# A twelve-stage decoder on one core: four more units per 32-head attention with plain out products

## What is computed

```
queries = rope(q @ Wq)            # 32 heads of 128
keys    = rope(k @ Wk)            # 8 heads of 128, each used by 4 query heads
values  = v @ Wv
scores  = queries @ keys.T / sqrt(128) + mask      # causal in layer 0
ctx     = softmax(scores) @ values
return ctx.reshape(B, S, 32 * 128) @ Wd            # 4096 columns to 512
x = layernorm(x + attention(x, context))
```

## Time and profile before

| | |
|---|---|
| median of 3 runs | 2799.91 us |
| lowest and highest | 2798.87 and 2800.82 us |
| the profiled execution, whole | 2801.92 us |
| its span | 2800.6 us (1.3 us lie around it) |
| mean granted TensorE clock | 0.987 of 2.4 GHz |
| first attention, main loop without a projection job, steps 56 to 66 | about 796 to 869 us |
| second attention, the same steps | about 1781 to 1853 us |

### The profile page before, as it was taken

How to read it: one execution, slowest core, us unless ns; L and a number is a source line. 1 busy time by engine, 2 the same in 40 slices (tenths; PEclk the granted TensorE clock), 3 DMA queues, 4 the chain that set the end, 5 groups by cost and what they waited for, 6 DMA issues and landing times.

```text
span 2800.6 us, 40463 instructions
## 1 busy us (share of the span) xinstructions
PE 2658.8 (95%) x15768; PEld 1764.9 (63%) x15768; DVE 1652.9 (59%) x3113; ACT 852.1 (30%) x2630; POOL 458.7 (16%) x511
## 2 busy tenths in 40 slices
PE   8999999999989899899999999899998898999998
PEld 7855666666665566556666666656774455576664
DVE  3557667776666456466676667664555644344455
ACT  0012222222233355222222222323444412333331
POOL 1022211222202100132122222022211121000002
PEclk9999999999999899999999999999999999999999
DMA  8631011100001100001111100010000010000000
GB/s 181 92 127 41 20 38 38 38 38 16 16 1 38 69 2 2 27 23 38 38 38 38 38 16 16 1 68 31 2 2 27 20 62 27 15 26 1 12 1 31
DMA packets 53821, 94.89 MB, mean 34 GB/s; under 512 B 29408, under 2 KB 38560, under 8 KB 47488
## 3 DMA queue, kind: packets, MB, share of 16 engines
q1 hardware_dynamic: 53632, 92.30, 10.8%
HBM read 83.89 MB, written 8.39 MB: 33 GB/s over the span
## 4 chain that ended last, share of the span: by engine, by line
PE 87%; DVE 7%; ACT 3%; issue 1%; DMA 1%; POOL 0%; DVEq 0%; SPq 0%; POOLq 0%; ACTq 0%
PE banks L628 19%; PE banks L666 13%; PE banks L620 4%; PE banks L687 4%; PE banks L1209 3%; PE banks L710 3%; PE banks L1719 3%; PE banks L303 3%; PE banks L1771 3%; PE banks L2009 2%; PE banks L2041 2%; PE banks L1748 2%; PE banks L2074 2%; PE banks L1724 2%; PE banks L650 2%; PE banks L697 2%
## 5 line engine op out<-in xcount | busy, mean ns | idle before, releaser
L628 PE MATMUL banks<-xT,weights 128*128 128x512 f32 x1024 | 458.2, 592 | 0.0
L748 ACT ACTIVATE E_x<-S_x,sm_x 128x128 f32<-128x128 f32 x512 | 199.3, 390 | 588.1 <-DVE sm_x L837 588.1
L628 PEld LDWEIGHTS banks<-xT,weights 128*128 128x128 f32 x1024 | 188.9, 190 | 209.5 <-issue 206.6
L887 POOL TENSOR_TENSOR QT<-QT,turned 128x512 f32<-128x512 f32 x128 | 162.4, 1269 | 708.2 <-DVE QT L781 506.5
L809 DVE TENSOR_TENSOR x<-banks,x 128x512 f32<-128x512 f32 x336 | 171.5, 510 | 143.7 <-PE banks L666 137.9
L779 DVE TENSOR_TENSOR turned<-banks,const 64x512 f32<-64x512 f32 x160 | 109.4, 684 | 233.1 <-PE banks L628 232.6
L666 PE MATMUL banks<-weights 128*128 128x256 f32 x896 | 223.8, 383 | 0.0
L161 POOL TENSOR_TENSOR norm_spread<-norm_mv,const 128x1 f32<-128x1 f32 x96 | 20.9, 218 | 1223.4 <-DVE norm_mv L157 1223.4
L666 PE MATMUL banks<-weights,OT 128*128 128x256 f32 x672 | 178.1, 387 | 25.1 <-DVE x L809 12.3
L666 PEld LDWEIGHTS banks<-weights 128*128 128x128 f32 x896 | 163.9, 191 | 44.4 <-DVE x L809 15.0
L666 PEld LDWEIGHTS banks<-weights,OT 128*128 128x128 f32 x672 | 120.5, 190 | 79.3 <-DVE x L809 38.8
(11 more groups left out here) (294 smaller groups left out, 4546.8 us busy)
## 6 DMA issues: line engine op xcount, KB each, us to landing
weights<-in_L_xwq SPq DMA_DIRECT2D x16, 1024.0 KB, 4.8
weights<-in_L_xwo SPq DMA_DIRECT2D x16, 1024.0 KB, 7.4
weights<-in_L_xwk SPq DMA_DIRECT2D x16, 256.0 KB, 5.1
weights<-in_L_xwv SPq DMA_DIRECT2D x16, 256.0 KB, 5.4
weights<-in_L_ffn_W_base SPq DMA_DIRECT2D x3, 1024.0 KB, 4.8
weights<-in_L_xwq SPq DMA_DIRECT2D x4, 768.0 KB, 5.0
weights<-in_L_xwo SPq DMA_DIRECT2D x4, 768.0 KB, 6.4
xT<-in_xT SPq DMA_DIRECT2D x4, 512.0 KB, 9.9
```

The source lines that it names most:

```text
L628: mm = PE.matmul(bank[:, :], weight, source[:, k, half_of(i)], start=k == 0, stop=k == KC - 1)
L748: ins = AC.activation(e[:, j, :], s[:, j, :], ACT.Exp, bias=sm[:, 0, j:j + 1], scale=1.0, accum_out=sm[:, 1, j:j + 1])
L887: PO.tensor_tensor(dst, dst, turned[j % 2][:, :, :], ALU.add).then_inc(*x_roped.one())
```

## The change

`pairs` goes from 28 to 26, for both attentions. Units 52 to 55, the last four of group 6, get plain products in steps 55 to 58 instead of the pairs 26 and 27 in steps 56 to 59. The other edits make this hold together: the plain product takes the `wo` buffer of its own group, SP's wait is written by `outs_to` (the same count as before for every group that is loaded), and the row statistics are taken for the last group alone.

```
-                pairs = (units - B) // 2
+                pairs = (units - B) // 2 - 2
...
                         if g >= 2:
-                            SP.wait_ge(*x_out(outs(4 * (g - 1))))
+                            SP.wait_ge(*x_out(outs_to(B * (g - 1) - 1)))
...
                         if u is not None:
-                            PE.wait_ge(*wo_here(G8 - 1))
+                            PE.wait_ge(*wo_here(u // B))
...
                             for h in range(4):
-                                mm = PE.matmul(psum[7][:, :], OT[u // 2 % 2][:, u % 2, h, :], wo[(G8 - 1) % 2][:, h, :], start=h == 0, stop=h == 3)
+                                mm = PE.matmul(psum[7][:, :], OT[u // 2 % 2][:, u % 2, h, :], wo[u // B % 2][:, h, :], start=h == 0, stop=h == 3)
...
                             DV.tensor_tensor(x[:, b, :], psum[7][:, :], x[:, b, :], ALU.add).then_inc(*x_sum.one())
-                            norm.stats(b, x_sum(NA * pairs + b + 1))
+                            if u >= units - B:
+                                norm.stats(b, x_sum(NA * pairs + u - 2 * pairs + 1))
```

## The result

The changed kernel takes 2779.14 us, the median of 6 runs (2775.44 to 2781.93), against 2799.46 us before (6 runs, 2798.87 to 2800.82). The ratio is 0.9925, with a 95% interval of 0.9913 to 0.9938. The direction was right, the size was not.

What follows compares the result with a forecast made beforehand. PE's list of work and its waits were taken to bound the kernel. Savings of 7.73 us in the first attention and 6.23 in the second, 13.96 together, took the median 2799.91 to 2786.0 us, range 2783.5 to 2790.

Steps and rivals of the forecast that it cites:

- The bound: Whole kernel: PE is busy 95% of the span, so the total is its work plus the places where it stands still.
- the place of the wait (L792): Step 56 of both attentions: PE idles 2.85 us until DVE's last sum of `OT`, with no projection job covering it.
- 4.28 us added to step 55: End of step 55: unit 52's plain product makes turn to scores 5.25 us instead of 0.97, so 4.28 us more.
- 22.5 us for steps 56 to 59: Steps 56 to 59, both attentions: four plain steps of 5.62 us each, without idle time on PE.
- no wait for L816: Steps 56 to 59: PE waiting for L816 there would show the forecast wrong; 1.01 us of slack was expected.
- First step that failed: Waits in both attentions: one slow stretch of 1.50 us per run, so 13.96 us saved in all.
- Second step: Clock in later blocks: one slow stretch more or fewer plus 0.5 us for the rest, 2 us either way.
- Half the gain: Rival: the eight new steps last 6.05 us each, giving back 3.4 us, total 2789.4 us; chance 0.10.
- The waits did not come back: Rival judged: steps keep 3.23 us of waits per pair, products cost their columns, total 2803.3 us; chance 0.03.
- chain through bank 7: Rival: new steps run without overlap, 8.94 us each, 12.6 us slower in all, total 2812.5 us; chance 0.02.
- given back behind: Rival: the block behind the first attention waits for something unmoved, losing 7.73 us, total 2793.7 us; chance 0.03.
- The rival made of the column rule: Plain products in the changed steps: 14% more by columns, 0.86 us more per pair, total 2803.3 us; chance 0.03.

Runs made afterwards that it cites:

- the shift runs: Kernel before plus one, two or three dummy matmuls at the end of step 59, second attention alone: 2795.01, 2799.55 and 2796.40 us, against 2800.25.
- e2: Kernel before with the change made in the second attention alone: 2785.13 us, ratio 0.9948; repeated on another chip, 2788.07 us.

## Why the prediction was wrong

**What held.** The bound (PE's list and its waits) and the place of the wait (L792) were right. The steps came as summed: 4.28 us added to step 55, 22.5 us for steps 56 to 59, no wait for L816. At full clock the two stretches together gave 2 x 6.23 = 12.46 us.

**First step that failed: "One in four such waits drew a slow stretch and a run has four of them, so one per run is the fair count."** It was 18 in 30. By 34.83 us in the mean, a stretch 56-60 of before costs 34.83 - 32.99 = 1.84 us over full clock, 3.7 for both attentions, where I had counted 1.50. The local gain is 2 x (34.83 - 26.76) = 16.1 us, not 13.96, which is 2.2 of the 6.4 us that were missing. Four places in one execution were too few to put a frequency on. I had seen the right quantity and its right price, 1.5 us each.

**Second step: "one more or one fewer, and 0.5 us for the rest, so 2 us either way."** I took the clock of the later blocks as noise about the same mean. By the profiles the bias and single-head blocks together lost 4.3 and 3.1 us (232.6 + 48.6 = 281.2 before, 276.9 and 278.1 after), and the shift runs show 2.4 to 6.4 us for moving them at all. 16.1 and 3.7 (the mean of the two) make 19.8 of the 20.3 us. The second term is the larger failure and the less certain one: that this change moved the later blocks to a better place, and not to a worse, stood nowhere in the trace of before, and why before's three profiles all show the bad one stays open.

**The rivals.** Half the gain needed steps of 6.05 us; they took 5.62. The waits did not come back, and no chain through bank 7 formed, with 1.2 us of slack. Nothing was given back behind: the blocks there took what they take in before's profiles, or less. The rival made of the column rule of the Trainium skill ("TensorE: Matmul & The Clock Gate", section "Back-to-back issue gap") had plain products dearer by 14% in columns. The comparison of three pairs with two bears out the trace's side: 14.68 against 14.71 us. By columns alone a pair would save 0.86 us: it has 512 fewer, and a plain product takes 3.44 us for 2048. In before's steps 54 and 55 the wait for L809 takes 0.55 us of that, since the start behind L710 comes 794.99 - 793.58 = 1.41 us later instead of 0.86. Three other starts around L666 come 0.1 us late each. Together that is the 0.86 us. The Trainium skill gives its figure in that section as the isolated gap of single matmuls; the waits between groups are not in it, and here they weigh as much as the columns.

No kernel run here is clearly ahead of the change; three plain pairs are level with it.

## What to carry to other kernels

A fast algorithm for a product pays only where its extra steps are covered; at the end of a pipeline, where the filler work has run out, the plain form can win although it has more columns. Cost a PE wait like the 2.85 us here at its length and the slow clock behind it, take the frequency of that from several executions, and leave room of several us, to both sides, for blocks that merely move in time. Before believing a gain of a few tenths of a percent, shift the kernel by a dummy instruction or two and see what that alone does.

## What the runs showed of the hardware

- A wait of 2.85 us on PE was followed by a stretch at half clock in 18 of 30 cases in the same code, at about 1.5 us each; with PE kept busy by dummies in it, in none of four (one profile).
- One added matmul of 0.86 us made a kernel of 2800 us faster by 5.2 us (ratio 0.9986 [0.9975, 0.9996]). In its profile the granted clock of blocks behind gave 1.7 us in the bias and 2.8 us in the single-head block.
- The same single-head block takes 48.6 to 48.7 us (eight profiles) or 45.9 us (five), with the clock at 0.50 at the same two places of the block or at none. How late in the span it starts does not tell which.
- The rotary block took between 222.5 and 231.8 us over the profiles, and 222.8 us in that of e2, where it is unchanged and ahead of every difference.
